# A message-passing layer on one core: padded list entries spread over 136 rows, list writes every fourth step, the transposes back in another bank, tags on GpSimd, and 32 unrolled steps on three engines

## What is computed

```python
h = relu(layernorm(x))                          # x: 100000 x 128 float32
msg_input = concat(h[src], h[dst])              # 50000 edges, sorted by dst, four types
for t in range(4):
    m = relu(msg_input @ W1[t] + b1[t]) @ W2[t] + b2[t]
    msgs = msgs + where(edge_type == t, m, 0)
agg = segment_sum(msgs, dst, 100000)
gi, gh = agg @ W_ih.T + b_ih, h @ W_hh.T + b_hh
r, z = sigmoid(i_r + h_r), sigmoid(i_z + h_z)
n = tanh(i_n + r * h_n)
out = x + (1 - z) * n + z * h
```

## Time and profile before

| | |
|---|---|
| median of 3 runs | 1870.78 us (1868.95 to 1872.88) |
| the profiled execution | 1868.72 us, its span 1866.8 us |
| busy share of the span | PE 89%, PEld 77%, VectorE 92%, ScalarE 81%, GpSimd 63% |
| HBM | 171 GB/s over the span |

### The profile page before, as it was taken

How to read it: one execution, slowest core, us unless ns; L and a number is a source line. 1 busy time by engine, 2 the same in 40 slices (tenths; PEclk the granted TensorE clock), 3 DMA queues, 4 the chain that set the end, 5 groups by cost and what they waited for, 6 DMA issues and landing times.

```text
span 1866.8 us, 43964 instructions
## 1 busy us (share of the span) xinstructions
PE 1667.9 (89%) x10181; PEld 1437.3 (77%) x10181; DVE 1709.5 (92%) x4382; ACT 1504.4 (81%) x3401; POOL 1177.8 (63%) x1982
## 2 busy tenths in 40 slices
PE   0135799999999999999999999999999999999798
PEld 0124688788888888888888888888888888887687
DVE  8596799999999999999999999999999999998687
ACT  0025798888888888989989899898998988988595
POOL 4777877887777566665666656666566665665320
PEclk9998899999999999999999999999999999999899
DMA  2225577776767777777777777777777776779653
GB/s 69 52 59 142 148 191 183 181 188 180 193 182 185 188 188 186 195 188 191 189 189 191 190 188 192 188 192 189 186 193 190 192 188 188 191 189 159 135 142 97
DMA packets 477053, 319.57 MB, mean 171 GB/s; under 512 B 106705, under 2 KB 463009, under 8 KB 476962
## 3 DMA queue, kind: packets, MB, share of 16 engines
q10 hardware_dynamic: 261792, 156.12, 28.0%
q1 hardware_dynamic: 185730, 106.99, 25.3%
q0 software_dynamic: 29440, 55.47, 13.1%
HBM read 211.65 MB, written 106.72 MB: 171 GB/s over the span
## 4 chain that ended last, share of the span: by engine, by line
PE 55%; ACT 4%; issue 4%; ACTq 2%; DMA 1%; DVE 1%; POOL 0%; SPq 0%; POOLq 0%; DVEq 0%
PE bank L1329 11%; PE bank L1331 9%; PE bank L1330 9%; PE bank L1409 8%; PE bank L1397 3%; PE bank L1389 3%; PE bank L1421 3%; PE bank L1420 3%; PE bank L1438 3%; PE bank L1448 3%; ACT n_zc L1284 1%; ACT n_h L1196 1%; ACT e_r L1272 1%; ACTq L1234 1%; ACTq L1213 1%
## 5 line engine op out<-in xcount | busy, mean ns | idle before, releaser
L577 POOL DMA_INDIRECT e_x<-in_x,rows_now x816 | 805.4, 987 | 247.5 <-issue 236.2
L1179 ACT ACTIVATE e_h<-e_x,shift,rstd 128x128 f32<-128x128 f32 x816 | 354.7, 490 | 92.0 <-DVE shift L1045 92.0
L1196 ACT ACTIVATE n_h<-n_x,shift,rstd 128x128 f32<-128x128 f32 x784 | 361.4, 488 | 2.4 <-issue 2.4
L1329 PE MATMUL bank<-n_h_hi,whh_hi 128*128 128x512 f32 x588 | 248.8, 423 | 29.3 <-ACT n_zc L1284 18.4
L1068 DVE TENSOR_SCALAR n_sel<-iota,n_rel 128x256 fp32r<-128x256 f32 x784 | 240.2, 368 | 32.1 <-POOL n_rel L628 31.7
L1409 PE MATMUL bank<-n_sel,n_win 128*128 128x256 f32 x1568 | 237.7, 294 | 29.9 <-DVE n_sel L1068 27.4
L1329 PE MATMUL bank<-n_a_hi,wih_hi 128*128 128x512 f32 x588 | 249.9, 425 | 0.0
L1331 PE MATMUL bank<-n_a_hi,wih_lo 128*128 128x512 f32 x588 | 233.0, 396 | 0.0
L1330 PE MATMUL bank<-n_h_lo,whh_hi 128*128 128x512 f32 x588 | 232.9, 396 | 0.0
L1331 PE MATMUL bank<-n_h_hi,whh_lo 128*128 128x512 f32 x588 | 232.8, 396 | 0.0
L1330 PE MATMUL bank<-n_a_lo,wih_hi 128*128 128x512 f32 x588 | 232.8, 396 | 0.0
(11 more groups left out here) (178 smaller groups left out, 4034.7 us busy)
## 6 DMA issues: line engine op xcount, KB each, us to landing
n_win<-messages SPq DMA_DIRECT2D x1568, 64.2 KB
messages<-e_msg ACTq DMA_DIRECT2D x204, 257.0 KB, 2.8
n_x<-in_x ACTq DMA_DIRECT2D x195, 256.0 KB
out<-n_out ACTq DMA_DIRECT2D x195, 256.0 KB
e_x<-in_x,rows_now POOLq DMA_INDIRECT x816
rows_now<-lists SPq DMA_DIRECT2D x204, 2.0 KB, 2.7
lists<-picks,list_rows POOLq DMA_INDIRECT x72
w<-in_W SPq DMA_DIRECT2D x1, 512.0 KB, 4.9
```

Of the source, the lines that this page charges most:

```text
L577: G.indirect_dma_start(e_x[:, s, 2 * end + t, :], None, x, bass.IndirectOffsetOnAxis(ap=rows_now[:, s, t, end:end + 1], axis=0)).then_inc( ...
L1179: last = A.activation(e_h[:, s % 2, k, :], e_x[:, s, k, :], ACT.Relu, scale=rstd[:, slot, col + k:col + k + 1], bias=shift[:, slot, col + ...
L1196: last = A.activation(n_h[:, s % 2, cols], n_x[:, s, cols], ACT.Relu, scale=rstd[:, slot, col + 4 + k:col + 5 + k], bias=shift[:, slot, co ...
L1329: T.matmul(o, w_hi, v_hi, start=start, stop=False)
```

## The change

Five things. The table `lists` is filled with row numbers 0 to 135, over and over, in place of zeros. The 24 later list halves are written every fourth step, at i % 4 == 0 from step 16, so that the last goes out at step 108 and no longer at step 62. The transposes back go to bank BHN in place of BA, with other waits. The tag copy goes from VectorE to GpSimd. And PE, VectorE and ScalarE have 32 steps written out ahead of the loop in place of 64, GpSimd 112, SyncE 128.

```diff
-HEAD = 64
+HEAD = 32
+WRITE_EVERY = 4
+WRITE_HEAD = 112
+LIST_HEAD = 128
@@ pipeline
-def pipeline(nc, eng, last, loop_end, step):
-    for i in range(0, HEAD):
+def pipeline(nc, eng, last, loop_end, step, head=HEAD):
+    for i in range(0, head):
@@ SyncE
                         if due(q - 7):
+                            sp.wait_ge(n_stats, q - 7)
                             sp.wait_ge(e_tagged, q - 7)
-                if isinstance(i, int) and i == HEAD - 1:
+                if isinstance(i, int) and i == LIST_HEAD - 1:
...
                             if half == 1 and t == 3 and within(g + LAG - 6, UNITS):
+                                sp.wait_ge(n_stats, g + LAG - 6)
                                 sp.wait_ge(e_tagged, g + LAG - 6)
@@ GpSimd
-            G.memset(zeros, 0).then_inc(s_zeroed, 1)
+            G.iota(spread_rows.rearrange("p (a n k) -> p a n k", a=3, k=2), pattern=[[0, 3], [1, TYPES * CAP // P // 3], [0, 2]],
+                   base=0, channel_multiplier=0).then_inc(s_spread, 1)
...
+            def wait_tags(q, m):
+                s = m % UNROLL
+                if within(q, UNITS) and due(q - 7):
+                    pool.wait_ge(e_stored[s], uses(q - 8, s, UNROLL, 16))
+
+            def write_tags(q, m):
+                s = m % UNROLL
+                if within(q, UNITS):
+                    G.tensor_copy(e_msg[:, s, :, TAG].bitcast(F32), rows_now[:, s, :, 1]).then_inc(e_tagged, 1)
...
-                if not isinstance(i, int) or i < WRITE_FROM or (i - WRITE_FROM) % 2:
+                if not isinstance(i, int) or i < WRITE_FROM or (i - WRITE_FROM) % WRITE_EVERY:
                     return None
-                h = 2 * TYPES + (i - WRITE_FROM) // 2
+                h = 2 * TYPES + (i - WRITE_FROM) // WRITE_EVERY
...
                     gather(i, m, (0,))
+                wait_tags(i - 4, m - 4)
                 relative_tags(i - LAG + 1, m - LAG + 1)
+                write_tags(i - 4, m - 4)
@@ VectorE
-                    V.tensor_tensor(n_out[:, s, :], n_xh[:, s, :], bank[BA][:], ALU.subtract).then_inc(n_outed, 1)
+                    V.tensor_tensor(n_out[:, s, :], n_xh[:, s, :], bank[BHN][:], ALU.subtract).then_inc(n_outed, 1)
...
-                q, s = i - 4, (m - 4) % UNROLL
-                if within(q, UNITS):
-                    if due(q - 7):
-                        dve.wait_ge(e_stored[s], uses(q - 8, s, UNROLL, 16))
-                    V.tensor_copy(e_msg[:, s, :, TAG].bitcast(F32), rows_now[:, s, :, 1]).then_inc(e_tagged, 1)
@@ TensorE
                     gate(BRZ, 0, s, "ha").then_inc(n_gate_r, 1)
-                    if due(g):
+                    if due(g - 1):
+                        pe.wait_ge(n_outed, g - 1)
+                    elif due(g):
                         pe.wait_ge(n_ted, g)
                     gate(BHN, 2, s, "h").then_inc(n_gate_hn, 1)
...
-                    if due(g - 2):
-                        pe.wait_ge(n_outed, g - 2)
-                    elif due(g):
+                    if due(g):
                         pe.wait_ge(n_alo, g)
...
-                    if within(g + 2, NG):
-                        pe.wait_ge(n_alo, g + 3)
+                    if within(g + 1, NG):
+                        pe.wait_ge(n_ted, g + 2)
                     elif due(g):
                         pe.wait_ge(n_outed, g)
                     for k in range(TILES):
-                        last = T.transpose(bank[BA][:, k * P:(k + 1) * P], n_e[:, s, k * P:(k + 1) * P], ident[:])
+                        last = T.transpose(bank[BHN][:, k * P:(k + 1) * P], n_e[:, s, k * P:(k + 1) * P], ident[:])
```

More of the change, by code:

```diff
@@ L62, in uses @@
     return (g - slot) * (inc // ring) + inc
-def pipeline(nc, eng, last, loop_end, step):
-    for i in range(0, HEAD):
+def pipeline(nc, eng, last, loop_end, step, head=HEAD):
+    for i in range(0, head):
         step(i, i % UNROLL)
-    with nc.Fori(HEAD, loop_end - UNROLL + 1, UNROLL, engines=[eng.engine], hint_back_edge=True) as i:
+    with nc.Fori(head, loop_end - UNROLL + 1, UNROLL, engines=[eng.engine], hint_back_edge=True) as i:
         for j in range(UNROLL):
@@ L209, in gnn_layer @@
         place, type_cols = (borrow(n_zc[:], at, ECOLS) for at in (0, ECOLS))
-        zeros = borrow(n_xh[:], ECOLS, TYPES * CAP * 2 // P).bitcast(I32)
+        spread_rows = borrow(n_xh[:], ECOLS, TYPES * CAP * 2 // P).bitcast(I32)
         passed = n_x[:].rearrange("p r w -> p (r w)")[:, 0:SEGMENTS * 4 * P].rearrange(
@@ L295, in gnn_layer @@
         s_ranked = sem("s_ranked")
-        s_zeroed = sem("s_zeroed")
-        s_cleared = sem("s_cleared")
+        s_spread = sem("s_spread")
+        s_padded = sem("s_padded")
         s_src = sem("s_src")
@@ L435, in _ @@
             sp.dma_start(dst_i[:], dst_cols).then_inc(s_dst, 16)
-            sp.wait_ge(s_zeroed, 1)
-            sp.dma_start(lists[0:TYPES * CAP, :].rearrange("(p c) k -> p (c k)", p=P), zeros).then_inc(s_cleared, 16)
+            sp.wait_ge(s_spread, 1)
+            sp.dma_start(lists[0:TYPES * CAP, :].rearrange("(p c) k -> p (c k)", p=P), spread_rows).then_inc(s_padded, 16)
             sp.dma_start(w1[:], W1.rearrange("t (k p) o -> p t k o", p=P)).then_inc(s_weights, 16)
@@ L530, in step @@
                                          ).then_inc(n_windowed[s], 16)
-            pipeline(nc, sp, LAST, LOOP_END, step)
+            pipeline(nc, sp, LAST, LOOP_END, step, LIST_HEAD)
             for s in range(4):
@@ L612, in _ @@
             G.tensor_tensor(gate_word[:, 0:1], g_power[0:1, 0:1], g_power[0:1, 0:1], ALU.add).then_inc(l_gated, 1)
-            pool.wait_ge(s_cleared, 16)
+            pool.wait_ge(s_padded, 16)
             for h in range(2 * TYPES):
@@ L688, in step @@
                     general_sums()
-            pipeline(nc, pool, LAST, LOOP_END, step)
+            pipeline(nc, pool, LAST, LOOP_END, step, WRITE_HEAD)
         @block.vector
```

## The result

| | before | after |
|---|---|---|
| median of 4 runs each, on one chip | 1869.87 us (1866.8 to 1872.88) | 1849.69 us (1848.93 to 1850.04) |
| ratio, 95% interval | | 0.9892 (0.9874 to 0.9909) |
| profiled execution, its span | 1868.72, 1866.8 us | 1848.93, 1847.0 us |

The change made the kernel 20.2 us faster, 1.1%. The prediction was 1843 us, range 1829 to 1857: the time lies 6.7 us above it, inside. The profiled execution gives the same difference, 1868.7 - 1848.9 = 19.8 us, so the two traces account for it.

What follows compares the result with a forecast made beforehand. A ring through PE, VectorE and ScalarE, all nearly full, was taken to set the pace, with a slower head and end. 1868.7 - 15.0 (head) - 2.7 (start) - 20.5 (end) + 12.6 (bank) = 1843.1 us; range 1829 to 1857.

Steps and rivals of the forecast that it cites:

- The bank: PE's weight load for BHN's product waits for n_out: 0.065 us a step over 194 steps, 12.6 us lost, bounds 0 and 23.
- the later of the prediction's two steps: Step with n_out ending at 1025.21: BHN's product starts as if 0.17 us late, moving the window sum 0.09 us.
- the load hides: Rival: BHN's weight load hides or the ring's slack takes it up, the bank costs nothing, 1830.5 us; chance 0.17.
- The head: Steps 20 to 65: spaced list writes ahead of the roots take back 15.0 of 16.7 us lost against the loop's pace.
- the writes keep their price: Rival: list writes from 16 to 108 each still delay one step, the head gains almost nothing, 1857 us; chance 0.08.
- The start: Before step 20: step 18's write goes, 3.9 us, less 1.2 for 15 tag copies; net 2.7 us gained, between 0.6 and 3.9.
- The end: Steps 199 to 207: padded entries no longer all fetch row 0; 95.4 becomes 74.9 us, 20.5 gained, bounds 10 and 23.
- a small region crowds too: Rival at the end: reads from a small region, not one address, keep 12 us or more, 1855 to 1863; chance 0.06.
- The tags in the loop: Tag copy leaves VectorE, where n_n hides it, for GpSimd, idle 38% of a step: counted at nothing.
- the fewer written-out steps: Fewer written-out steps on three engines: counted at nothing, as the loop's own pace is the reference already.
- The longer ring: Rival: the wait for n_out closes a longer ring, PE stands at BHN 0.26 us a step, 1880 us; chance 0.04.

## Why it came out so, step by step

**The bank: right in cause, near in size.** The prediction took 0.065 us a step and 12.6 us from a load that isn't early. PE's rows after, gate r's and BHN's first matmuls and the window sum in two steps, and the loads:

```profile
1005.88 0.47 PE L1342 MATMUL bank<-n_h_hi,whh_hi 128*128 128x512 f32 x1
...
1007.36 0.46 PE L1342 MATMUL bank<-n_h_hi,whh_hi 128*128 128x512 f32 x1
1007.65 0.39 PE L1343 MATMUL bank<-n_h_lo,whh_hi 128*128 128x512 f32 x1
...
1008.90 1.19 PE L1422 MATMUL bank<-n_sel,n_win 128*128 128x256 f32 x8
...
1014.41 0.47 PE L1342 MATMUL bank<-n_h_hi,whh_hi 128*128 128x512 f32 x1 [0.32 <-ACT n_zc L1297]
...
1015.94 0.50 PE L1342 MATMUL bank<-n_h_hi,whh_hi 128*128 128x512 f32 x1
1016.28 0.40 PE L1343 MATMUL bank<-n_h_lo,whh_hi 128*128 128x512 f32 x1
...
1017.54 1.20 PE L1422 MATMUL bank<-n_sel,n_win 128*128 128x256 f32 x8
```

```profile
1007.31 0.19 PEld L1342 LDWEIGHTS bank<-n_h_hi,whh_hi 128*128 128x128 f32 x1 [0.23 <-DVE n_out L1072]
...
1015.94 0.19 PEld L1342 LDWEIGHTS bank<-n_h_hi,whh_hi 128*128 128x128 f32 x1 [0.33 <-DVE n_out L1072]
```

From BHN's first matmul to the second it is 0.29 and 0.34 us where it was 0.23. In the second step the start is late as well, 1.53 instead of 1.47 behind gate r; together 0.06 + 0.11 = 0.17, the figure worked out for the later of the prediction's two steps. Not all of it reaches the window sum. Over steps 84 to 195 the window sum starts on average 0.07 us later behind gate r than before. The kernel with only this part lost 0.083 us a step, the changed kernel against the one with it undone 0.080; the changed loop against the one of before 0.061. On the whole kernel it is 14 to 16.5 us where 12.6 was taken. It is well inside the bounds of 0 and 23, and it is the clearest lesson here: with it undone the same change is worth 34 us (0.9818).

The prediction set against this the rule of the Trainium skill ("TensorE: Matmul & The Clock Gate", section "Architectural detail: the array is 16× 32×32, not 1× 128×128") that a matmul can begin before its weight load has completed. By that rule the load that waits would cost nothing. The matmul is indeed recorded at the load's own start in the row at 1015.94, but the next one starts 0.34 us behind it. The measurement decides: 0.08 us a step is paid, the begun matmul doesn't give it back, and the rival "the load hides" (1830.5) is out.

**The head: right.** -15.0 plus 46 x 0.065 = 3.0 for the bank is 12.0 gained; measured 11.6. The spread writes alone gave 14.9, against 15.0. The reason given was half right. It named two things: the place (ahead of the roots) and the spacing (one write, not two, in a cycle of four steps). The place is worth 5.5 us over all 24 writes, the spacing about 20 in the head, with the tags on GpSimd. The rival that the writes keep their price (0.8 us each) is out in either place: 0.23 at most.

**The start: the step that failed, by 2.3 us.** Step 20 came 0.4 us earlier, not 2.7. The write of step 18 went, and the casts cost 0.09 each against 0.08. The term that failed is "`iota` for `memset` over 816 elements is below 1 us and beside SyncE's loads". It took 2.19 us, 1.42 more than the fill before, and what stands behind it on GpSimd isn't hidden: VectorE's first cast waits for the constants that follow it. So the first list write starts 1.2 us later and the first gather 1.4 (57.22 for 55.82); at step 4 it is 1.6. The fourteen casts up to step 18 add 1.5 (184.16 for 181.14), some 0.3 more than taken. Less the write's 3.85, step 19's `n_rel` is 0.8 us earlier, and step 20's `n_d` 0.4. This chain of GpSimd's issues, without gaps, passed on what was put ahead of it.

**The end: right in cause, 3.5 us too much in size.** 16.4 gained where -20.5 + 0.6 was taken. The packets fell to 118 ns (near 130 was named), and the rival that a small region crowds too is refuted even for eight rows. The prediction put the whole excess down to the packets; some of it may have gone with the granted clock, 0.91 before and 1.00 now, which no run separates from them. But these nine steps take 79.0 and not 75.5 us. Steps 199, 201 and 205 take 10.7, 9.1 and 9.7 us. In the first of them, with no DMA waited for, ScalarE and GpSimd stand where the profile shows no releaser:

```profile
1713.36 0.59 ACT L1271 ACTIVATE n_h_hi<-bank 128x512 fp32r<-128x512 f32 x1
1716.48 0.60 ACT L1273 ACTIVATE n_a_hi<-bank 128x512 fp32r<-128x512 f32 x1 [2.52 <-issue]
```

```profile
1717.23 0.18 POOL L589 TENSOR_TENSOR gate_word<-g_power 1x1 f32<-1x1 f32 x1 [7.07 <-issue]
```

It is where the engines leave the loop for the written-out rest, and the queue that carries instructions has six packets between 1710 and 1720 us:

```profile
q14 instruction: 6, 0.05, 1.3%
```

That this is a fetch of code is argued from these rows and was not tried. Against it: the kernel with the padded entries alone leaves its loop at the same step, and its step 199 takes 8.1 us (its long one, 11.8, is step 202). The stalls of steps 201 and 205 stay open too. The prediction priced the nine steps at the loop's own pace, which leaves such costs out.

**The tags in the loop and the fewer written-out steps: both counted at nothing, and not quite so.** The loop took 1098.7 to 1099.7 us in the three kernels with the old bank, 64 written-out steps and the tags on VectorE. It took 1095.9 with the tags on GpSimd alone, and 1095.1 to 1096.2 in all four kernels with the old bank and 32 written-out steps, wherever the tags were. So either of the two gives some 3 us, and both together give no more. Why is open. The fewer written-out steps were not tried alone. At their new loop entry nothing stands out: the steps about step 32 take 8.6 and 8.8 us, others of the head up to 9.1.

What was missed on the tags is a price of their own while the writes are dense: 6.3 us in the head. With the writes spaced and the old bank it is gone (385.0 with them on GpSimd, 386.2 without). This is one reason why the parts alone don't add up: -0.57, -0.89, +0.56 and +0.20% sum to -0.70%, where the whole is -1.08%. The written-out steps, which were not among the four, are the other candidate.

**The sum, and some luck in it.** The longer ring, the rival on the slow side (0.26 us a step), is out with 0.08 measured. Against the terms, in us: start +2.3, head +0.4, loop -0.6, end +3.5, the last steps -0.2 (0.3 lost where 0.5 was counted for the bank), and 0.3 between the last `n_d` and the span's end. These make 5.7 above the 1843.1 forecast; measured were 1848.9. The loop's -0.6 is two misses that cancel: the bank cost 10.5 us there and not 8.6, and the 2.5 to 3 us above came back unforeseen.

## What to carry to other kernels

Here a wait on a PE weight load was paid although its semaphore came just in time (0.08 us a step, some 15 us in all), so put such a wait behind work that doesn't need it. For an engine that is idle a third of the time, ask over which stretch that time lies: work spread evenly over a cycle was nearly free, the same work twice as dense cost 20 us. Entries that only pad a gather should name different rows. And a fill at the head of a chain without gaps has to be costed: it took 1.2 us here.

## What the runs showed of the hardware

- BHN's weight load, behind other 128x512 matmuls, starts 0.23 us ahead of its own when it waits for nothing. With a semaphore met just in time the lead is 0.02 us, and 0.08 us a step is lost. Behind transposes, with no wait, the lead is 0.03 us as well and nothing is lost.
- Queue 0's packets (2 KB each) took 548 ns while the padded entries of its gathers all named one row of `x`; with 136 rows they took 118 and with 8 rows 120.
- On GpSimd at the start, an `iota` over 128 x 816 int32 takes 2.19 us, a `memset` of the same size 0.77.
- A VectorE cast of 128 x 256 int32, alone 0.29 us, took 2.06 us while GpSimd's `iota` ran, and ended 0.15 behind it. The Trainium skill says in "SBUF — State Buffer", section "Who interferes with whom", that a cast can take the ports that VectorE shares with GpSimd, and that whoever comes first keeps them for its whole instruction. By that rule the cast stands until the `iota` is through; the trace agrees. The cast of 128 x 1 just ahead of it, at 2.78, was not held up by the same `iota` (0.15 us).
